# One edge portion prepared before an expert's sums instead of behind them, and a query feature kept in its PSUM bank

## What is computed

```python
xn = layernorm(x)
x = x + rgcn(xn, src, dst, edge_type, edge_weight) + linear_attention(xn)
f = layernorm(x)
h1 = relu(einsum('bsd,edh->bseh', f, expert_w1) + expert_b1)
h2 = relu(einsum('bseh,ehf->bsef', h1, expert_w2) + expert_b2)
expert_out = einsum('bsef,efo->bseo', h2, expert_w3) + expert_b3
x = x + sum over the two best experts of expert_out * routing weight
```

## Time and profile before

| | us |
|---|---|
| median of 3 runs | 3184.87 (3183.43 to 3185.27) |
| the profiled execution's own time | 3181.19 |
| its span, first to last instruction | 3179.7 |
| PE busy | 2914.3 (92%) |
| VectorE busy | 2350.3 (74%) |
| ScalarE busy | 2013.7 (63%) |
| GpSimd busy | 1745.7 (55%) |
| mean granted TensorE clock | 0.984 of full |

### The profile page before, as it was taken

One profiled execution on the slowest core, in us unless ns is written; L12 is line 12 of the kernel. 1 busy time (PEld: TensorE's weight loads), 2 busy tenths in 40 slices (PEclk: granted clock), 3 DMA queues, 4 the chain that ended last, 5 costly groups with the idle time before them and its releaser, 6 DMA issues.

```text
span 3179.7 us, 48059 instructions
## 1 busy us (share of the span) xinstructions
PE 2914.3 (92%) x16807; PEld 2506.8 (79%) x16808; DVE 2350.3 (74%) x5404; ACT 2013.7 (63%) x3996; POOL 1745.7 (55%) x1696
## 2 busy tenths in 40 slices
PE   5999999897789999999999999999999999999998
PEld 4888888786678787888878888877888887878887
DVE  3479655423678888888888888888788888888885
ACT  3555556453567666666766767666666676666664
POOL 1000000003477777777777777777777777777750
PEclk8999999998999999999999999999999999999999
DMA  6676555556444444444343444434344443334420
GB/s 233 255 269 226 197 217 207 205 201 246 143 129 124 119 115 119 123 123 124 116 124 111 120 123 125 123 116 123 109 123 122 125 123 116 114 118 123 123 84 10
DMA packets 179841, 456.72 MB, mean 144 GB/s; under 512 B 46604, under 2 KB 104918, under 8 KB 159405
## 3 DMA queue, kind: packets, MB, share of 16 engines
q0 software_dynamic: 80352, 219.14, 23.9%
q1 hardware_dynamic: 97074, 232.64, 20.2%
q10 hardware_dynamic: 2172, 1.85, 0.2%
HBM read 296.01 MB, written 158.29 MB: 143 GB/s over the span
## 4 chain that ended last, share of the span: by engine, by line
PE 28%; POOL 21%; DVE 14%; issue 8%; ACT 3%; DMA 2%; DVEq 1%; SPq 0%; ACTq 0%; POOLq 0%
POOL ring L1157 21%; PE bank L1644 18%; DVE row_lo L1391 6%; PE acc L1698 5%; ACT row_hi L1214 2%; DVE sel L1385 2%; DVE y L1529 1%; DMA ring<-y_tab,tab 1%; ACT bank L1229 1%; DVE h_lo L1468 1%; PE bank L1782 1%; PE acc L1707 1%; PE bank L1671 1%; PE acc L1644 1%; DVE xn_c L1489 1%
## 5 line engine op out<-in xcount | busy, mean ns | idle before, releaser
L1157 POOL DMA_INDIRECT ring<-y_tab,tab x1666 | 1731.3, 1039 | 599.5 <-issue 491.8
L1228 ACT ACTIVATE h_hi<-bank,bias_t 128x512 fp32r<-128x512 f32 (+1 forms) x600 | 407.4, 679 | 500.9 <-PE bank L1644 475.0
L1214 ACT ACTIVATE row_hi<-ring,tab 128x256 fp32r<-128x256 f32 x1666 | 702.1, 504 | 18.8 <-issue 18.8
L1391 DVE SCALAR_TENSOR_TENSOR row_lo<-ring,tab,row_hi 128x256 fp32r<-128x256 f32 x1666 | 684.3, 476 | 22.5 <-ACT row_hi L1214 19.5
L1698 PE MATMUL acc<-row_hi,sel 128*128 128x256 f32 x1666 | 435.0, 297 | 157.4 <-DVE row_lo L1391 157.4
L790 PE MATMUL yb<-wr_hi,xhl 128*128 128x512 f32 x1568 | 510.7, 398 | 31.6 <-ACT yst L351 25.6
L1468 DVE TENSOR_TENSOR h_lo<-bank,h_hi 128x512 fp32r<-128x512 f32 (+1 forms) x600 | 388.4, 673 | 150.8 <-ACT bank L1229 147.1
L1698 PEld LDWEIGHTS acc<-row_hi,sel 128*128 128x128 f32 x1666 | 319.2, 192 | 224.3 <-DVE row_lo L1391 221.7
L351 ACT ACTIVATE yst<-yb 128x512 f32<-128x512 f32 x392 | 230.5, 595 | 321.0 <-PE yb L790 284.0
L1698 PE MATMUL acc<-row_lo,sel 128*128 128x256 f32 x1666 | 412.8, 283 | 0.0
L1229 ACT ACTIVATE bank<-bank,bias_t 128x512 f32<-128x512 f32 (+1 forms) x600 | 387.1, 645 | 0.0
(11 more groups left out here) (271 smaller groups left out, 5324.6 us busy)
## 6 DMA issues: line engine op xcount, KB each, us to landing
y_tab<-yst SPq DMA_DIRECT2D x97, 1024.0 KB, 3.9
ring<-y_tab,tab POOLq DMA_INDIRECT x1666, 2.8
xt_tab<-xhl SPq DMA_DIRECT2D x25, 1024.0 KB, 3.9
xc<-xt_tab SPq DMA_DIRECT2D x25, 1024.0 KB, 5.3
x<-x_tab SPq DMA_DIRECT2D x49, 256.0 KB, 3.5
xs<-in_x SPq DMA_DIRECT2D x24, 512.0 KB, 6.0
x_tab<-xs SPq DMA_DIRECT2D x24, 512.0 KB, 5.0
out<-y SPq DMA_DIRECT2D x24, 512.0 KB
```

Of the source, the lines that this page charges most:

```text
L1157: pool.indirect_dma_start(out=out_ap, out_offset=None, in_=y_tab[:, :], in_offset=bass.IndirectOffsetOnAxis(ap=idx_ap, axis=0)).then_inc(s ...
L1214: last = act.activation(row_hi[:, p % BUFS, q, :], ring[:, p % SLOTS, q, :], ACT.Copy, scale=tab[:, n % 2, t, k, 2:3])
L1228: act.activation(dest[:, m, 0:W], b[:, 0:W], ACT.Relu, bias=bias)
L1391: last = dve.scalar_tensor_tensor(out=row_lo[:, p % SLOTS, q, :], in0=ring[:, p % SLOTS, q, :], scalar=tab[:, n % 2, t, k, 2:3], in1=row_h ...
```

## The change

VectorE's `prepare` of the portion that PE sums behind h2(e+1), which is portion 5, 7 or 9, moves from behind the sums of expert e to ahead of them, for e = 1, 2 and 3. The other portions stay. For the query, ScalarE writes the relu back into its bank instead of into `rq`, and signals a new semaphore `q_set`; VectorE reads that bank and is now the engine that frees it, so PE's denominators wait for the bank to be freed and `qf_ready` is gone.

```diff
-            q_items = [("q", m, "act") for m in range(KC)]
+            q_items = [("q", m, "dve") for m in range(KC)]
...
                         act.activation(eq[:, m, :], b[:, 0:NS], ACT.Exp, bias=bias_t[:, BQ + m:BQ + m + 1])
-                        gone(act.activation(rq[:, m, :], b[:, 0:NS], ACT.Relu, bias=bias_t[:, BQ + m:BQ + m + 1]))
+                        act.activation(b[:, 0:NS], b[:, 0:NS], ACT.Relu, bias=bias_t[:, BQ + m:BQ + m + 1]).then_inc(q_set, 1)
...
                     for k in range(KC):
-                        dve.wait_ge(*done(i, plan, "q", k))
-                        dve.scalar_tensor_tensor(out=qf[:, k, :], in0=eq[:, k, :], scalar=1.0, in1=rq[:, k, :],
-                                                 op0=ALU.min, op1=ALU.add).then_inc(qf_ready, 1)
+                        dve.wait_ge(q_set, KC * (i + 1) + k + 1)
+                        gone(dve.scalar_tensor_tensor(out=qf[:, k, :], in0=eq[:, k, :], scalar=1.0,
+                                                      in1=bank[plan["q", k][0]][:, 0:NS], op0=ALU.min, op1=ALU.add))
...
+                        early = e + 1 in BEHIND_H2
+                        if more and early and between(e + 1) < parts(i + 1):
+                            prepare(i + 1, between(e + 1))
                         if e == 0:
                             dve.wait_ge(y_stored, 16 * (i + 1))
                         else:
                             dve.drain()
...
-                        if more and between(e + 1) < parts(i + 1):
+                        if more and not early and between(e + 1) < parts(i + 1):
                             prepare(i + 1, between(e + 1))
...
                     b = give(i, plan, "den", 0)
-                    pe.wait_ge(qf_ready, KC * (i + 1) + KC)
+                    pe.wait_ge(*done(i, plan, "q", KC - 1))
```

More of the change, by code:

```diff
@@ L1004, in gps_layer @@
             emptied = {"act": sem("act_emptied"), "dve": sem("dve_emptied")}
-            qf_ready, rden_ready, acc_full, x1_done = (sem(n) for n in ("qf_ready", "rden_ready", "acc_full", "x1_done"))
+            rden_ready, acc_full, x1_done = (sem(n) for n in ("rden_ready", "acc_full", "x1_done"))
             var_c, std_c, xn_c, d_ready, ex_ready, gap_ready, g2_ready, gate_ready = (
@@ L1008, in gps_layer @@
             y_ready, y_stored, xc_in, x1_in = (sem(n) for n in ("y_ready", "y_stored", "xc_in", "x1_in"))
-            ft_hi_set, h_set = (sem(n) for n in ("ft_hi_set", "h_set"))
+            ft_hi_set, h_set, q_set = (sem(n) for n in ("ft_hi_set", "h_set", "q_set"))
             w_in = [sem(f"w{i}_in") for i in range(3)]
```

## The result

The change makes the kernel slower: 3210.65 us (3204.57 to 3214.27, four runs) against 3184.15 (3181.95 to 3185.27, four runs) for the kernel before beside it, a ratio of 1.0084 with an interval of 1.0072 to 1.0095. The forecast was 3193.5 in a range of 3179 to 3212. So the direction was right and the size too small: 26.5 us lost, 0.8%, where 8.6 were forecast. The profiled execution of after took 3204.57 us, the lowest of the four; its mean granted clock was 0.972 of full, against 0.984 before.

The account below looks back on a forecast made before the run. PE's 139.0 us of waits for VectorE's low rows in the loop were what the change touches; -3.5 us of gain and +12.1 of clock falls gave +8.6 on 3184.87, so 3193.5 us, range 3179 to 3212.

Parts of the forecast that it names:

- The pairs: PE's waits for portions 5, 7 and 9 move to 6, 8 and 10, which hang on ScalarE; gain only 3.5 us.
- the 4 us of 139 that were allowed: Sign: PE's idle time put down to VectorE's low rows in the loop stays within some 4 us of 139.
- The 0.15 us a pass at portion 10: VectorE's second `h_lo` of h2(4) begins 0.15 us sooner, and portion 10 with it: 3.5 us over 23 passes.
- The size of the waits: PE's new waits ahead of portions 6, 8 and 10: 2.03, 1.4 and 1.77 us.
- The falls: PE's clock falls behind portion 6's new wait as often as behind b3: 8.6 x 1.40 = 12.1 us lost.
- the first rival: Portion 10's wait of 1.77 us sets off falls too, another 12.1 us: 3205.6 us; chance 0.26.
- second step: Clock falls behind portion 6's wait only; wrong if it never falls behind a wait, or falls behind both kinds.
- the prediction's upper bound: Behind portion 6, a fall in each of the 14 passes without one behind b3: 19.6 us lost.
- The query: Relu written back into its bank, read there by VectorE: between 0 and 0.2 us more, taken as zero.
- That no fall follows: Second rival: the loop's waits only change places and the clock never falls behind them: 3181.4 us; chance 0.21.
- The third rival: Waits for portions 5, 7 and 9 go and don't come back: 76.4 us gained, 3108.5; chance 0.10, part included.

Follow-up runs that it names:

- experiment 7: Kernel after, with ScalarE's high rows of portions 6, 8 and 10 made ahead of its work on h2: 3130.21 us, ratio 0.9834.
- experiment 2: Kernel before with only the query's change (relu written back into its bank), portions at their old places: 3181.49 us, ratio 0.9997.
- experiment 3: Kernel after, with six useless matmuls ahead of portion 6 and six ahead of portion 10: 3177.84 us, ratio 0.9982.
- experiment 9: Kernel before (no move, old query) with ScalarE's high rows of portions 6, 8 and 10 made early: 3155.66 us, ratio 0.9911.
- experiment 1: Kernel before with only the moves of portions 5, 7 and 9, the query as before: 3213.52 us, ratio 1.0093.
- experiment 10: Kernel before with b3 taken apart, each half right behind its half of w3(1): 3188.88 us, ratio 1.0015.

## Why the prediction was right, and where its size failed

**The pairs.** Right at all three. The waits of 5, 7 and 9 went, those of 6, 8 and 10 took their place, and the idle time for low rows is 140.4 us, within the 4 us of 139 that were allowed. The releaser named, ScalarE's second half of h2, is the one: experiment 7 takes it away and the gain comes. The 0.15 us a pass at portion 10 is there, as 0.13 (93.15 against 93.28; 2.8 us over 22 passes, where 3.5 were forecast over 23).

**The size of the waits.** Too small by 0.1 to 0.3 us: 2.30, 1.53 and 2.08 us came out against 2.03, 1.4 and 1.77. I had added the old wait at a portion to the wait that was moved there. But PE gains more than the wait itself when it doesn't wait: in the pass of after shown above, the first matmul of portion 6, behind a wait, takes 0.39 us and the next starts 0.23 later, while the first of portion 5, without a wait, takes 0.27 and the next starts 0.12 later (1607.22). And a wait is counted from the end of the matmul before it, though matmuls that are 0.39 us long start 0.23 apart when nothing holds them up, 0.16 ahead of that end. So PE comes to the second of a pair 0.11 + 0.16 = 0.27 us sooner still, which is what is missing at portion 6.

**The falls.** That waits of about 2 us bring the clock down in this loop, as b3's low rows do, was right, and it is the reason for the sign. The term that was mis-sized is the falls behind portion 10: forecast none, measured 10 x 1.74 = 17.4 us. This was the first rival, 3205.6 us, and it is what happened. The prediction had named falls behind both kinds of waits as the sign that its second step is wrong, and by that sign it was. That 3210.65 us lies inside the range is owed to the part of this rival that the range took in; the forecast by itself went to 3201. The rival was refused by a comparison of 1.77 us with 1.69 and 1.99; with 2.08 the same comparison would have taken it. Behind portion 6, 8.6 x 1.40 = 12.1 us were forecast and 6 x 1.55 = 9.3 measured. That these are near each other is partly luck: the count was taken over from b3, but what came is a fall in every one of the 22 passes that has none behind b3, the prediction's upper bound, and there were six such passes and not 14, since the falls behind b3 grew from 9 to 16. The sum didn't have that growth, which costs 0.5 us.

**The query.** Right: nothing (experiment 2).

**The other rivals.** That no fall follows (3181.4) is what the useless matmuls bring about (3177.84), so it was the right price for the wrong case. The Trainium skill, "TensorE: Matmul & The Clock Gate", section "HAM oscillation — how this bites in real kernels", looks for longer idle gaps than these. The traces differ: 16 falls in after stand behind idle times of 2.06 to 2.30 us, and filling the gaps removes them all. The third rival (the waits really go) needed ScalarE earlier; with that the moves gain 25 us, not the 76.4 that it was given, since portions 6, 8 and 10 keep 0.58 to 1.36 us of wait and 15 falls of 1.5 us each stand behind b3.

## What to carry to other kernels

When two waits hang on a chain, making the first one's data earlier moves its wait to the second; look for what the second hangs on and move that as well, or neither. Waits that are put together can cost more than the same waits apart, when PE idles long enough in one for its clock to fall: so compare the longest single idle gap, not only the sum, and count it to the new arrival, without the slow start behind the old wait. Where such a gap can't be closed, a few matmuls into a bank that is free anyway keep the clock, and cost nothing that experiment 3 can tell while they fit into it.

## What the runs showed of the chip that I had not expected

**Useless work makes the kernel faster.** Two times 1.52 us of matmuls whose result is thrown away take a pass from 94.66 us on average to 93.40, and the kernel from 3210.65 to 3177.84 us.

**A fall changes where the next one comes.** The falls behind b3 rose from 9 to 16 although b3 stands where it stood, and went back to 9 with the gaps at portions 6 and 10 filled. A wait of 2.30 us at portion 6 was followed by a fall in all six passes of after that had none behind b3, but not in three passes with 5 moved alone, nor in the first pass of after; one of 2.06 to 2.09 us at portion 10 in 10 passes of 22. In experiment 9, with a pass of 92.2 us and b3 in one piece, only two falls are left. And in experiment 1 one fall stands behind a wait of 1.78 us at portion 6. The length of a gap alone doesn't decide; what does stays open.

**A split has a price on PE.** Two pieces of four matmuls with 6 rows take 1.13 + 1.12 us where one of eight takes 1.99, and with the slow start behind each it is 0.38 us in the pass shown, enough to use up the falls it removes (experiment 10).
